# Inverse transform of the second token half written as sums and differences by TensorE, in a fused perceiver block

## The reference, cut to what matters

```python
x = x + xattn(layernorm(x), ctx, ctx, mask, ...)
x = x + mixing(layernorm(x), Wq, bq, Wk, bk, Wv, bv)
x = x + experts(layernorm(x), W1, W2, Wg, bg)

def mixing(x, ...):
    q, k, v = x @ Wq + bq, x @ Wk + bk, x @ Wv + bv
    s = sum over tokens of irfft(rfft(k) * rfft(v))
    return irfft(rfft(s) * conj(rfft(q)))
```

## Time and profile before

| | |
|---|---|
| median of 3 runs | 815.13 us (815.08 to 815.38) |
| the profiled execution's own time | 810.39 us |
| its span in the trace | 808.3 us |
| mean granted TensorE clock | 0.982 of full speed |
| TensorE (PE) busy | 773.9 us, 96% of the span |
| VectorE (DVE) busy | 625.0 us, 77% |
| ScalarE (ACT) busy | 470.1 us, 58% |
| GpSimd (POOL) busy | 241.2 us, 30% |

### The profile page before, as it was taken

One profiled execution on the slowest core, in us unless ns is written; L12 is line 12 of the kernel. 1 busy time (PEld: TensorE's weight loads), 2 busy tenths in 40 slices (PEclk: granted clock), 3 DMA queues, 4 the chain that ended last, 5 costly groups with the idle time before them and its releaser, 6 DMA issues.

```text
span 808.3 us, 22182 instructions
## 1 busy us (share of the span) xinstructions
PE 773.9 (96%) x8851; PEld 461.5 (57%) x8851; DVE 625.0 (77%) x990; ACT 470.1 (58%) x847; POOL 241.2 (30%) x413
## 2 busy tenths in 40 slices
PE   8987999999999999999999999996899999999995
PEld 3444455554455554455556545555868867876783
DVE  5877888888887887777768668787797879788860
ACT  4634656647665656665647034246478668766950
POOL 0143344332454333443322200004053323242220
PEclk9999999999999999999999999997799999999998
DMA  8335253444233443234423511102899998988500
GB/s 305 140 116 108 51 146 80 107 107 81 66 84 90 107 107 75 86 86 127 122 55 56 210 50 56 53 0 92 278 353 411 410 378 324 369 330 327 223 31 15
DMA packets 94901, 125.56 MB, mean 155 GB/s; under 512 B 76352, under 2 KB 79168, under 8 KB 83956
## 3 DMA queue, kind: packets, MB, share of 16 engines
q1 hardware_dynamic: 92260, 117.65, 45.6%
q0 software_dynamic: 2576, 7.02, 2.4%
HBM read 100.47 MB, written 6.88 MB: 133 GB/s over the span
## 4 chain that ended last, share of the span: by engine, by line
PE 79%; DVE 12%; ACT 3%; DMA 3%; issue 1%; POOL 1%; SPq 0%; POOLq 0%; DVEq 0%; ACTq 0%
PE bank L1470 58%; PE bank L1841 10%; PE bank L1632 4%; DVE arena L931 3%; PE bank L1813 3%; PE bank L1598 3%; ACT arena L696 2%; DMA arena<-arena 2%; DVE arena L987 2%; DVE arena L993 1%; ACT arena L663 1%; DMA arena<-in_wv_t 1%; DVE arena L1009 1%; PE bank L1800 1%; DVE arena L963 1%
## 5 line engine op out<-in xcount | busy, mean ns | idle before, releaser
L1470 PE MATMUL bank<-arena 128*128 128x160 f16 (+6 forms) x3992 | 572.7, 304 | 9.9 <-DVE arena L931 3.8
L1470 PEld LDWEIGHTS bank<-arena 128*128 128x128 f16 (+1 forms) x3992 | 327.8, 100 | 243.1 <-issue 12.0
L663 ACT ACTIVATE arena<-arena 128x256 f16<-128x256 f32 (+5 forms) x302 | 254.0, 889 | 23.6 <-PE bank L1813 10.1
L931 DVE SCALAR_TENSOR_TENSOR arena<-arena 128x2048 f16<-128x2048 f32 (+4 forms) x102 | 201.1, 1991 | 32.0 <-ACT arena L663 31.5
L663 ACT ACTIVATE arena<-bank 128x512 f16<-128x512 f32 (+1 forms) x175 | 100.1, 585 | 149.5 <-PE bank L1470 112.3
L931 DVE SCALAR_TENSOR_TENSOR arena<-bank,arena 128x512 f16<-128x512 f32 (+1 forms) x174 | 116.7, 682 | 48.3 <-ACT arena L663 44.7
L1841 PE MATMUL bank<-arena 128*128 128x512 f16 x384 | 86.6, 379 | 0.0
L696 ACT ACTIVATE arena<-arena 128x257 f32<-128x257 f32 x128 | 63.5, 498 | 26.3 <-DVE arena L995 26.3
L532 POOL TENSOR_TENSOR arena<-arena 32x1024 f16<-32x1024 f32 (+1 forms) x16 | 34.1, 2133 | 143.7 <-PE bank L1632 143.5
L1841 PEld LDWEIGHTS bank<-arena 128*128 128x128 f16 x384 | 36.2, 98 | 41.1
L549 POOL COPY arena<-arena 32x256 f16 (+1 forms) x128 | 50.3, 393 | 24.0 <-DVE arena L931 11.8
(11 more groups left out here) (110 smaller groups left out, 467.1 us busy)
## 6 DMA issues: line engine op xcount, KB each, us to landing
arena<-in_w SPq DMA_DIRECT2D x64, 1024.0 KB, 7.6
arena<-in_ctx_t SPq DMA_DIRECT2D x15, 1024.0 KB, 5.5
arena<-in_awt SPq DMA_DIRECT2D x3, 1024.0 KB, 7.1
l_dram<-arena SPq DMA_DIRECT2D x4, 512.0 KB, 3.8
x_dram<-arena SPq DMA_DIRECT2D x1, 2048.0 KB, 14.4
arena<-in_wk_t SPq DMA_DIRECT2D x4, 256.0 KB, 4.9
arena<-in_ctx_t SPq DMA_DIRECT2D x4, 256.0 KB, 5.7
arena<-in_wv_t SPq DMA_DIRECT2D x1, 1024.0 KB, 8.7
```

What stands on the lines that cost most here:

```text
L663: return a.activation(dst, src, ACT.Copy, scale=scale)
L931: return v.scalar_tensor_tensor(dst, src, scale, h, ALU.mult, ALU.subtract)
L1470: last = m.matmul(out_ap, w, x, start=(n == 0), stop=(n == len(pairs) - 1))
```

## The change

For the second half of the tokens, TensorE writes the finished 512 positions of a tile. Even part: each of the two matmuls streams `idft` twice (a broadcast over the two halves), 512 columns, into the whole bank. Odd part: each chunk is multiplied twice with 256 columns, by `idft` into the left half and by a new constant `idft_minus` (its rows with the sign turned, 256 KB) into the right half, on top of the even part. VectorE then adds the whole bank to x in one instruction. The first half is as before. `mask_bias` moves to another region of SBUF, and `idft_minus` takes its place in the region that is kept.

```diff
-        mask_bias = keep.take([L], F32)
+        idft_minus = keep.take([2, NF], F32)
...
+        mask_bias = xa.take([L], F32)
...
                     sp.dma_start(idft, i["idft"]).then_inc(s["idft_landed"], 16)
+                    sp.dma_start(idft_minus, i["idft_minus"]).then_inc(s["idft_landed"], 16)
...
                 bank = (BA, BB, BE, BF)[t % 4]
+                if t >= HT:
+                    dve.wait_ge(s["irfft_ps"], t + 1)
+                    v.tensor_tensor(x_tok[:, t, :], x_tok[:, t, :], bank[:], ALU.add).then_inc(s["x2_done"], 1)
+                    dve.wait_ge(s["x2_done"], t + 1)
+                    return v.bn_stats(stats[:, t, :], x_tok[:, t, :])
...
+            def back_both(t, parity):
+
+                pe.wait_ge(s["x2_done"], from_zero(t - 3))
+                pe.wait_ge(s["unbound"], 2 + parity + 1)
+                for c in (2 * parity, 2 * parity + 1):
+                    w = spec[1][1][:, c, t % HT * P:(t % HT + 1) * P]
+                    bank = (BA, BB, BE, BF)[t % 4]
+                    if parity == 0:
+                        last = m.matmul(bank[:].rearrange("p (h n) -> p h n", h=2), w,
+                                        idft[:, c:c + 1, :].broadcast_to((P, 2, NF)), start=(c == 0), stop=False)
+                    else:
+                        for h, rows in enumerate((idft[:, c, :], idft_minus[:, c - 2, :])):
+                            last = m.matmul(bank[:, h * NF:(h + 1) * NF], w, rows, start=False, stop=(c == KC - 1 and h == 1))
+                return last
...
-            pe.wait_ge(s["idft_landed"], 16)
+            pe.wait_ge(s["idft_landed"], 32)
...
             for t in range(HT, NT):
-                back(t, 0)
+                back_both(t, 0)
             for t in range(HT, NT):
-                back(t, 1).then_inc(s["irfft_ps"], 1)
+                back_both(t, 1).then_inc(s["irfft_ps"], 1)
...
+        "idft_minus": np.ascontiguousarray(chunks(-inv[:, :NF].astype(np.float32))[:, 2:]),
```

## The result

| | before | with the change |
|---|---|---|
| median of timed runs | 815.21 us (815.08 to 815.38, 4 runs) | 820.15 us (819.5 to 821.21, 4 runs) |
| ratio | | 1.0057, 95% interval 1.0043 to 1.0071 |
| span of the profiled execution | 808.3 us | 817.7 us |

The change makes the kernel 4.9 us slower. The forecast was +6.2 us, 821.3, with a range of 818.4 to 822.7: right in direction and inside the range, 1.2 us above the measured median. The two spans can't be set against each other: the profiled execution of the kernel before took 810.39 us, 4.8 under the median of its timed runs, while that of the changed kernel (819.5 us) lies among them. In a later job (one series of runs on one chip), in which the kernel before had a median of 810.84 us, the changed kernel came to 816.08: +5.2 us, ratio 1.0072 (1.0058 to 1.0085).

What follows compares the result with a forecast made beforehand. TensorE, busy 96% of the span, was taken as the bound, with two equal chains leaving the changed stretch. Even parts 2.65 and odd parts 3.52 us made +6.17: 815.13 + 6.2 = 821.3 us, range 818.4 to 822.7.

Steps and rivals of the forecast that it cites:

- Two tied chains: At GpSimd's power of group 6, VectorE's chain and the one over TensorE's transposes and ScalarE tie to 0.03 us.
- Price of a pass: TensorE's f32 passes: 0.22 us for 256 columns, 0.44 for 512, because columns pace the array.
- Rival 1: On TensorE, weight loads pace wide passes, so even parts stay hidden: +3.5 us, 818.7; chance 0.05.
- rival 3: On TensorE from 542 us, unbroken f32 passes run closer together and hide even parts: +0.7 us, 815.8; chance 0.04.
- VectorE: Second-half additions: 0.78 us saved per tile, used up by later deliveries; group 6 ready near 559.1, 0.8 later.
- The fixed sequence behind the transposes: From transposes through copies, normalising, power, gate and gather, nothing else releases work, so all moves by 6.17 us.
- Clock: TensorE's clock drop from transposes into gather stays in place relative to the transposes: 0 in the sum, spread 0.6 either way.
- rival 2: Longer unbroken TensorE work keeps the clock up through transposes and gather, returning 2.1 us: +4.1 us, 819.2; chance 0.08.
- The rest of the kernel: From the first expert on, TensorE works without a pause worth the name, so the delay reaches the end whole.
- the 6.17 us: Delay of the start of TensorE's transposes behind the odd parts, from 549.88 to 556.05 us.
- My sign of being wrong: An expert part shorter than 231 us from its start to the end of the span would show the forecast wrong.
- The load of the new constant: Loading `idft_minus` costs SyncE one more issue, 0.43 us at 399.3, covered until 410.81: nothing added.

Runs made afterwards that it cites:

- after_again: The changed kernel, unedited, run and traced again in a later job: 816.08 us, ratio 1.0072 to the kernel before.
- pe_alone: The changed kernel with TensorE's side kept, VectorE's old three instructions per tile and no second round of experts: ratio 1.0065 to the kernel before.
- even_alone: The changed kernel with wide even parts, odd parts written to the left half only, no second round of experts: ratio 1.0022 to the kernel before.
- odd_alone: The changed kernel with doubled odd parts, even parts written to the left half only, no second round of experts: ratio 1.0025 to the kernel before.
- before_again: The kernel before, unedited, a second execution with a trace: 811.92 us, with 811.33 us as that job's median.
- dve_alone: The kernel before with only VectorE's single addition for tiles 4 to 7, and no second round of experts: ratio 1.0002.
- before_moved: The kernel before with the same move of transposes, copies and normalising as after_moved: ratio 1.001.
- after_moved: The changed kernel with transposes of tiles 0 to 3 issued between pairs of odd parts, ScalarE's copies likewise split: 812.33 us, ratio 1.0022 to the kernel before.

## Why the prediction was right, point by point

**Two tied chains.** Right. VectorE decided by a little more than I read: 0.15 us and not 0.03, since GpSimd starts the power slightly before the recorded end of the low part.

**Price of a pass.** Right: 0.434 us for a pass of 512 f32 columns, predicted 0.44; 0.216 for 256 in a row of 32, predicted 0.22. The odd parts start 6.95 us after the even ones where it was 546.36 - 541.97 = 4.39, so 2.56 later, predicted 2.65; of the 3.43 us added (6.95 - 3.52) the wait covered 0.87, as predicted. The shift of the transposes is 5.94 us for 6.17. Rival 1 (weight loads pace the passes) and rival 3 (closer passes when unbroken) are refuted by the same rows. The Trainium skill's page "TensorE: Matmul & The Clock Gate", section "Back-to-back issue gap", gives about 131 ns per matmul of 512 columns in a stream with weight loads. The traces of this case do not agree: 96 passes of 512 f16 columns took 0.218 us each, and an unbroken row of 32 f32 passes of 256 columns kept 0.216.

**VectorE.** Right in what decides: 0.78 us saved per tile and none of it seen. It ended 5.6 us before the power (559.24, 564.88), predicted "some 5". The wait of about 0.4 us per tile did not come out: it was 0.24 for tile 5 and nothing for tiles 6 and 7, which cost nothing off the path.

**The fixed sequence behind the transposes.** Right by the interval to the normalising of tile 4 (4.36 us in the kernel before and in the changed one), and shown to be the cause by moving it.

**Clock.** I put nothing into the sum and gave 0.6 either way, and 2.1 to rival 2. From gather to first expert it is 7.38 us in the first trace of the changed kernel for 8.03, 0.65 at most, but the kernel before has 7.59 in its second trace, so little or none of that is the change's. The last transposes stayed at the lower clock (1.03 us for eight, as before), so rival 2 is out.

**The rest of the kernel.** The term that was mis-sized. That the 6.17 us "reach the end whole" was wrong by about 1 us: I had set aside the pause of 0.65 us in the second expert as not worth a name, and by the later traces it is a piece of slack of 0.65 to 1.47 us, gone in the changed kernel. With the shift itself (0.2 too large) that is more than enough for the 1.2 us by which the sum stood too high; the first job has no trace of the kernel before at its own level to show the split there. My sign of being wrong, an expert part shorter than 231 us, did come true in after_again and pe_alone (229.9), by that pause and not by a mechanism that I had in mind. It was also badly set: the kernel before itself has 808.3 - 577.46 = 230.8.

**The load of the new constant.** Right: 0.43 us on the queue at 400.01, landed in 5.5 us, and the next issue there only at 411.48. No run has this load or the move of `mask_bias` alone; even_alone and odd_alone have both, and their times are explained to some 0.2 us without them, with intervals of 0.7 either way.

## What to carry to other kernels

When a chain of waits runs through an engine, look for a second chain that ends at the same instruction before crediting the engine with its savings: an in-order queue (here GpSimd's power behind a low part) is such a meeting place. Work moved to TensorE cost its columns at once, here 0.216 us for an f32 pass of 256 columns where an f16 pass has 512 in 0.218, and what stands in line behind it pays, even on engines that are idle. Issuing short work that others wait for between the long passes gave back 3.75 us of 5.2 without removing anything.

## What the runs showed of the hardware that was not expected

The pause in the second expert goes with the instruction queue. The profile's page lists a queue "q8 instruction" with 44 packets, 16 KB each. In every trace with a pause, TensorE stops behind one and the same matmul of its program, the 5783rd (the 5784th in odd_alone), and goes on 1.5 to 1.6 us behind the end of one of these packets. Times in us from the start of the span:

```
kernel         packet ends   pause ends   difference
before         608.92        610.42       1.50
before_again   610.66        612.27       1.61
dve_alone      609.18        610.65       1.47
even_alone     611.34        612.88       1.54
before_moved   610.36        611.94       1.58
odd_alone      612.03        613.63       1.60
```

The traces without a pause there fit. In them TensorE comes to the matmul behind that place (the 5785th) more than those 1.6 us after the end of the packet:

```
kernel         packet ends   matmul starts   difference
pe_alone       611.70        614.51          2.81
after_again    611.69        614.52          2.83
after          611.99        614.38          2.39
after_moved    608.52        611.78          3.26
```

From before to after_again the packet comes 2.8 us later, but the experts start 5.95 us later (583.41, 577.46). In after_moved the experts start earlier than in odd_alone (580.66, 582.20) and there is still no pause, because the packet comes 3.5 us earlier; so it is not simply a later start that removes it, and why the packet comes when it does is open. That TensorE waits for instructions whose load competes with the weights (the DMA engines' share is 1.01 from 600 to 620 us in the kernel before) fits all ten traces, but no run isolated it. That is also how a kernel that reaches its experts later can lose less than its delay.
